# More all-ones filler products ahead of the prefix sums and ahead of tile 0's gather in an expert-routing kernel

## Chip, cores and metric

The kernel runs on one core of a Trainium2 chip. The metric is the device time of one execution in microseconds (us); lower is better. The engines that matter here are PE (TensorE, the matrix engine; PEld is its weight load), DVE (VectorE), ACT (ScalarE), POOL (GpSimd, which also issues the indirect transfers) and SP (which issues the plain ones).

## What is computed

A graph network of three levels on 625 nodes with 256 features, and then a mixture of experts on its result:

```python
x = x + gnn(layernorm(x), edge_index, ...)          # three edge convolutions, 20000 edges
xn = layernorm(x)
gate_scores = xn @ Wg + bg                          # 625 x 8
_, idx = top_k(gate_scores, 2)
mask = one_hot(idx, 8).sum(axis=-2)
h = gelu(einsum('td,edh->teh', xn, W1) + b1)        # 8 experts, 256 -> 512
y = einsum('teh,ehd->ted', h, W2) + b2              # 512 -> 256
out = x + einsum('ted,te->td', y, mask)
```

The kernel doesn't compute all eight experts for every node. It computes only the two that a node picks: it sorts the picks by expert into tiles of 128 rows ("slots"), gathers the rows of each tile, runs the tile's expert on it, and adds the result to the output rows.

## The kernel before, in words

Nodes are held as 5 tiles of 128. The program is written out by hand for each engine. Each engine runs its own list in order, and semaphores (`wait_ge`, `then_inc`) tie the lists together. All that stands in a list behind a waiting instruction waits too.

The last level of the graph part ends with `g_product` (lines 1340 to 1342, dense products). After it the routing stretch begins, some 14 us of small steps in which PE, DVE and ACT take turns. PE's list there is, in order:

- transposes of `x1_sb` (L1578) and the gate products of 8 columns (L1585), with `keep_clock(WARM_GATE)`, 6 fillers, between them;
- `keep_clock(WARM_ROUTE)`, fillers, at line 1601;
- a wait for `both_ready`: DVE has found the two best experts of each node (`best`, `best_id`, `pick`, `both_bf`, L1213 to L1223);
- the prefix sums: ten bf16 products of 8 to 40 columns (L1604, L1608, L1611) that count how many nodes ahead of each picked the same expert;
- `keep_clock(WARM_GATHER)`, fillers, at line 1652;
- `gather(0)` (L1622): 20 float32 products of 128 columns, which collect the rows of slot tile 0 with one-hot matrices (`hot_slot`) that DVE makes from the prefix sums (L1231 to L1240). It waits for `x2_f_done` (ACT has normalised the rows) and `hot_ready`;
- a wait for `experts_ready`, then a load of two expert numbers into PE's registers (L407), and `up(0, 0)` (L1629), the first expert product, which waits for `xt_ready`: ACT has copied the gathered tile from PSUM (L874);
- `gather(1)`, the same 20 products for slot tile 1, and a second load of expert numbers;
- `transpose_h(0)` (L1642), and ten products (L1665) that turn the slots into row numbers for the indirect transfers;
- the expert loop: per tile `transpose_h` (L1642), `up` (L1629), `transpose_x` (L1636), `down` (L1648), with each tile's rows fetched by an indirect transfer of POOL (L634) and its results added to the output by another (L640). Ten tiles are written out, the rest come from a loop with a run-time count.

The fillers are products whose result nobody reads. They go to `bank[3]`, which nothing uses in this stretch:

```python
def keep_clock(n):
    for _ in range(n):
        pe.matmul(bank[3][:, 0:P], ones_bf[:], ones_bf[:], start=True, stop=True)
...
keep_clock(WARM_ROUTE)
pe.wait_ge(both_ready, 1)
...
keep_clock(WARM_GATHER)
pe.wait_ge(x2_f_done, NT)
gather(0)
```

They wait for no semaphore, so PE starts them as soon as what stands ahead of them has been issued; what stands behind them waits until they are through.

## Time and profile before

| | us |
|---|---|
| median of 3 timed runs | 176.64 |
| the three runs | 175.98, 176.64, 177.07 |
| the profiled execution's own time | 177.76 |
| its span, first to last instruction | 175.9 |

The profile describes one execution. What lies around its span is 177.76 - 175.9 = 1.86 us. A duration from the trace is set against 177.76 us, not against the median. Rows give the start and length in us from the span's start, the engine, the source line, output and inputs, and the count of instructions. The granted clock (PEclk) is a share of full speed: 1.00 is 2.4 GHz and 0.50 is 1.2 GHz.

### The profile page before, as it was taken

How to read it: one execution, taken by the hardware profiler on the slowest of the kernel's cores; microseconds unless marked ns; L12 is line 12 of the kernel's file. 1: busy time of each engine (PE TensorE's matmuls, PEld its weight loads, DVE VectorE, ACT ScalarE, POOL GpSimd, SP SyncE). 2: the span in 40 equal slices, each digit the busy share in tenths (PEclk: the TensorE clock that was granted, in tenths of full speed). 3: DMA queues.
4: the chain of work that ended last, by engine and by line, in shares of the span. 5: the costliest groups of instructions: out<-in, count | busy, mean ns of one | idle time of the engine just before them, and what ended most of it. 6: DMA issues, size and time to landing. Idle time of an engine off the chain costs nothing.

```text
span 175.9 us, 3014 instructions
## 1 busy us (share of the span) xinstructions
PE 144.8 (82%) x958; PEld 121.4 (69%) x959; DVE 92.2 (52%) x245; ACT 63.9 (36%) x182; POOL 72.2 (41%) x95
## 2 busy tenths in 40 slices
PE   1443394999998899999999698989999999999710
PEld 1332273998798899999999686856666666766600
DVE  6699789768799891344139781622222222223100
ACT  8333975467212140312122640323433333343200
POOL 6605430000499049960001100075555666663661
PEclk9999997599999999999999958999999999999995
DMA  4679999996000699300000450024243333332332
GB/s 147 201 165 368 371 365 267 172 384 229 9 4 0 201 317 347 102 6 0 0 0 4 157 192 6 0 63 89 37 77 66 63 60 60 60 60 34 60 60 30
DMA packets 16983, 21.24 MB, mean 121 GB/s; under 512 B 1794, under 2 KB 13316, under 8 KB 16836
## 3 DMA queue, kind: packets, MB, share of 16 engines
q1 hardware_dynamic: 13764, 16.79, 29.4%
q0 software_dynamic: 3200, 4.20, 14.6%
q8 instruction: 12, 0.20, 0.4%
q14 instruction: 7, 0.06, 0.1%
HBM read 17.72 MB, written 3.26 MB: 119 GB/s over the span
## 4 chain that ended last, share of the span: by engine, by line
PE 58%; DVE 16%; DMA 11%; issue 5%; POOL 3%; ACT 2%; POOLq 1%; SPq 1%; ACTq 0%; DVEq 0%
PE cnt_ps L1648 9%; PE bank L1629 6%; DMA x_sb<-in_x 5%; PE bank L1505 4%; PE g_ps L1629 4%; PE cnt_ps L1642 3%; PE cnt_ps L1505 3%; PE bank L1622 3%; PE g_ps L1340 2%; PE g_ps L1341 2%; PE g_ps L1342 2%; DMA out_rows<-y_sb,row_of 2%; DVE a_hi L1038 2%; DMA out_rows<-y_sb,row_put 2%; DVE hot_lo L955 2%
## 5 line engine op out<-in xcount | busy, mean ns | idle before, releaser
L1648 PE MATMUL cnt_ps<-w_sb,h_t 128*128 x104 | 24.7, 380 | 1.2 <-ACT h_t L870 1.2
L1648 PEld LDWEIGHTS cnt_ps<-w_sb,h_t 128*128 128x128 f32 x104 | 18.8, 190 | 3.9 <-issue 1.9
L640 POOL DMA_INDIRECT out_rows<-y_sb,row_of x10 | 15.9, 1591 | 12.7 <-DMA out_rows<-y_sb,row_of 10.1
L634 POOL DMA_INDIRECT xg<-x_rows,row_of x12 | 12.0, 997 | 20.7 <-DVE row_of L1309 17.4
L1396 PE MATMUL bank<-hot_key,hot_lo 125*128 125x45 bf16 (+4 forms) x80 | 8.3, 244 | 11.2 <-DVE hot_key L958 7.2
L955 DVE TENSOR_TENSOR hot_lo<-iota_lo,edge_rel 125x1024 bf16<-125x1024 int16 x20 | 13.8, 690 | 3.0 <-PE g_ps L1396 2.9
L1396 PEld LDWEIGHTS bank<-hot_key,hot_lo 125*128 125x128 bf16 x80 | 5.2, 123 | 13.6 <-DVE hot_key L958 11.7
L1278 DVE TENSOR_TENSOR y_sb<-cnt_ps,b_bc 128x256 f32<-128x256 f32 x13 | 5.5, 425 | 17.3 <-PE cnt_ps L1648 17.3
L1629 PE MATMUL bank<-w_sb,xt 128*128 x28 | 13.4, 600 | 0.7 <-ACT xt L874 0.5
L1274 DVE TENSOR_TENSOR h_pre<-bank,b_bc 128x512 f32<-128x512 f32 x7 | 4.8, 692 | 16.0 <-PE bank L1629 16.0
L866 ACT ACTIVATE h_act<-h_pre 128x512 f32<-128x512 f32 x13 | 8.2, 629 | 9.7 <-DVE h_pre L1274 9.7
L1629 PE MATMUL g_ps<-w_sb,xt 128*128 x24 | 11.4, 596 | 0.0
L602 POOL IOTA key_tables<- 128x720 int16 x1 | 1.8, 1789 | 22.9 <-DVE a_hi L1038 22.9
L870 ACT COPY h_t<-cnt_ps 128x512 f32<-128x512 f32 x13 | 7.6, 585 | 9.7 <-PE cnt_ps L1642 9.6
L861 ACT COPY xt<-bank 128x256 f32<-128x256 f32 x12 | 4.5, 372 | 16.4 <-PE bank L1636 16.4
L1505 PE MATMUL bank<-a_hi,ys_hi 128*128 128x384 f32 x30 | 10.1, 338 | 0.0
L580 POOL TENSOR_TENSOR w_lo<-w_stage,w_hi 128x512 fp32r<-128x512 f32 x7 | 10.0, 1450 | 0.2
L1505 PE MATMUL bank<-a_hi,ys_lo 128*128 128x384 f32 x30 | 10.1, 336 | 0.0
L1396 PE MATMUL g_ps<-hot_key,hot_lo 125*128 125x45 bf16 (+4 forms) x80 | 8.5, 245 | 1.7 <-ACT a_hi L720 0.9
L1274 DVE TENSOR_TENSOR h_pre<-g_ps,b_bc 128x512 f32<-128x512 f32 x6 | 4.2, 692 | 10.5 <-PE g_ps L1629 10.5
L958 DVE TENSOR_TENSOR hot_key<-key_tables,edge_rel 125x360 bf16<-125x360 int16 (+4 forms) x20 | 8.9, 446 | 0.0
L1134 DVE SCALAR_TENSOR_TENSOR ut_lo<-bank,ut_hi 128x384 fp32r<-128x384 f32 x4 | 2.2, 558 | 12.5 <-ACT ut_hi L840 12.5
(289 smaller groups left out, 407.4 us busy)
## 6 DMA issues: line engine op xcount, KB each, us to landing
w_sb<-in_L_ffn_W SPq DMA_DIRECT2D x16, 512.0 KB, 9.6
b_bc<-in_L_ffn_b SPq DMA_DIRECT2D x8, 256.0 KB, 4.9
w_stage<-in_L_gnn_W SPq DMA_DIRECT2D x3, 512.0 KB, 5.7
w_stage<-in_L_gnn_Wf SPq DMA_DIRECT2D x4, 256.0 KB, 7.6
b_bc<-in_L_ffn_b SPq DMA_DIRECT2D x1, 1024.0 KB, 9.1
x_sb<-in_L_gnn_bf POOLq DMA_DIRECT2D x1, 640.0 KB, 14.3
x_rows<-x_f SPq DMA_DIRECT2D x1, 640.0 KB, 3.3
x_sb<-in_x SPq DMA_DIRECT2D x1, 512.0 KB
```

Of the source, the lines that this page charges most:

```text
L580: pool.tensor_tensor(w_lo[:, r, :, i * D:(i + 1) * D], part, w_hi[:, r, :, i * D:(i + 1) * D].bitcast(f32), ALU.subtract)\
L634: pool.indirect_dma_start(out=xg[:, b, :], out_offset=None, in_=x2_rows, in_offset=bass.IndirectOffsetOnAxis(ap=rows, axis=0)).then_inc(x_ ...
L640: pool.indirect_dma_start(out=out, out_offset=bass.IndirectOffsetOnAxis(ap=rows, axis=0), in_=y_sb[:, b, :], in_offset=None, compute_op=AL ...
L866: act.activation(h_act[:, h, :], h_pre[:, h, :], ACT.Gelu).then_inc(act_ready, 1)
L870: act.copy(h_t[:], bank[2].rearrange("p (k s) -> p k s", k=HC)).then_inc(h_t_ready, 1)
L955: dve.tensor_tensor(hot_lo[:, u % RING:u % RING + 2, :, :], iota_lo[0:EP].unsqueeze(1).broadcast_to((EP, 2, P, CT)), rel[:, 0].unsqueeze(2 ...
L958: dve.tensor_tensor(hot_keys(u, 2), turn_keys(u // UNROLL)[0:EP].rearrange("p n w i -> p (n w) i").unsqueeze(1) .broadcast_to((EP, 2, NT * ...
L1274: dve.tensor_tensor(h_pre[:, h, :], up_bank(h)[:, :], b1_bc[:, ds(e, 1), :], ALU.add).then_inc(pre_ready, 1)
L1396: last = pe.matmul(pane(k), hot_lo[:, u % RING, :, i], hot_keys(u)[:, 0, :, i], start=i == i0, stop=i == i0 + n_i - 1, skip_group_check=True)
L1505: step = pe.matmul(z_bank(i), y[:, u, m], a_t[:, u, cols], start=first and u == 0 and y is y_parts[0], stop=u == NT - 1 and y is y_parts[- ...
L1629: last = pe.matmul(up_bank(h)[:, :], xt[:, k, h * P:(h + 1) * P], w1_sb[:, ds(e, 1), k, :], start=k == 0, stop=k == KC - 1)
L1648: last = pe.matmul(bank[3][:, 0:D], h_t[:, k, :], w2_sb[:, ds(e, 1), k, :], start=k == 0, stop=k == HC - 1)
```

## The change

Two of the three counts of fillers grow: 40 in place of 22 ahead of the prefix sums, and 28 in place of 14 ahead of tile 0's gather. The six between the gate products stay. Nothing else differs.

```diff
-WARM_GATE, WARM_ROUTE, WARM_GATHER = 6, 22, 14
+WARM_GATE, WARM_ROUTE, WARM_GATHER = 6, 40, 28
```

## Rows read from the trace of the kernel before

**Rows 1.** The page: span, PE's busy tenths and the granted clock in 40 slices

```profile
span 175.9 us, 3014 instructions
PE   1443394999998899999999698989999999999710
PEclk9999997599999999999999958999999999999995
```

**Rows 2.** Chain that ended last, 100.5 to 108.2 us: start, length, what

```profile
100.54 0.21 DVE both_bf L1223
100.75 0.05 issue
100.80 0.21 PE bank L1604
101.01 0.09 PE bank L1608 x4
101.10 0.15 PE bank L1611 x5
...
102.33 0.57 DVE hot_slot L1240
102.90 0.14 issue
103.03 4.51 PE bank L1622 x20
...
107.56 0.38 ACT xt L874
107.94 0.13 issue
```

**Rows 3.** Chain that ended last, 108 to 113 us

```profile
108.07 1.98 PE bank L1629 x4
110.05 2.23 PE g_ps L1622 x20
```

**Rows 4.** Windows: stretch, length, busy of each engine, granted clock, DMA share, GB/s

```profile
99.40:100.40 1.00, 0.03 (x1) 0.00 (x0) 0.93 (x12) 1.00 (x4) 0.00 (x0) 1.00 0.18 52
100.40:100.50 0.10, 0.00 (x0) 0.00 (x0) 0.10 (x1) 0.10 (x2) 0.00 (x0) 0.74 0.15 51
103.00:107.20 4.20, 4.17 (x19) 4.20 (x20) 3.15 (x19) 0.00 (x0) 0.00 (x0) 0.50 0.42 146
107.30:107.60 0.30, 0.23 (x2) 0.03 (x1) 0.00 (x0) 0.04 (x1) 0.00 (x0) 1.00 0.00 0
```

**Rows 5.** PE's timeline around both runs of fillers

```profile
98.04 1.39 PE L1347 MATMUL cnt_ps<-ones_bf 128*128 128x128 bf16 x22
100.80 0.21 PE L1604 MATMUL bank<-both_bf,tri_bf 128*128 128x40 bf16 x1 [1.37 <-DVE both_bf L1223]
101.09 1.65 PE L1347 MATMUL cnt_ps<-ones_bf 128*128 128x128 bf16 x14
```

**Rows 6.** Windows in earlier stretches with gaps on PE, columns as in rows 4

```profile
29.00:32.00 3.00, 1.88 (x14) 1.88 (x14) 3.00 (x7) 0.78 (x4) 0.00 (x0) 0.50 1.14 215
56.00:60.00 4.00, 2.82 (x18) 2.62 (x17) 3.78 (x12) 0.81 (x2) 1.25 (x1) 1.00 0.26 78
```

**Rows 7.** PE's timeline at the gap of the second of them

```profile
57.81 0.45 PE L1340 MATMUL bank<-ut_hi,w_hi 128*128 128x384 f32 x1 [1.18 <-DVE ut_lo L1134]
```

**Rows 8.** DVE's timeline after the first one-hot matrices

```profile
104.85 0.13 DVE L1265 TENSOR_SCALAR pairs_i<-owner_i 1x1 int32<-1x1 int32 x1
105.17 0.82 DVE L1240 TENSOR_TENSOR hot_slot<-iota_p,place 128x640 f32<-128x640 f32 x1
106.17 0.18 DVE L1286 CAST tile_pos<-tile_pos_i 128x20 bf16<-128x20 int32 x1
```

**Rows 9.** Register loads and POOL's wait: duration ns min/median/max, first and last start

```profile
L407 PEldq TENSOR_LOAD <-owner_i x2: 553/1368/2183, 105.0 to 110.1; - x2
L630 POOLq EVENT_SEMAPHORE  x1: 17/17/17, 107.0 to 107.0; - x1
```

**Rows 10.** Chain that ended last, 105 to 176 us

```profile
114.65 2.85 DMA xg<-x_rows,row_of
...
155.75 0.44 DVE y_sb L1278
...
156.97 3.82 DMA out_rows<-y_sb,row_of
```

## The prediction

> **What bounds the kernel now.** I read the page first. Its clock line is 9 nearly everywhere and drops at two places, slices 7 and 8 and slices 24 and 25 [rows 1]. The second drop is where the change sits, because a slice is 4.4 us and the routing stretch lies at 94 to 108 us. Then I read the chain that ended last, since only time on it is worth anything. In the routing stretch it runs DVE (`both_bf`), the prefix sums on PE, DVE again (`hot_slot`), then 4.51 us of PE for `gather(0)`, then the copy of the tile on ACT [rows 2]. The fillers aren't on it at all. The same 20 products appear once more as `gather(1)`, and there the chain gives them 2.23 us [rows 3]. The windows say why: the clock is 1.00 until 100.4, falls to 0.50 there after a stretch in which PE was busy for 0.03 of 1.00 us, stays at 0.50 while the gather keeps PE full (4.17 of 4.20 us), and is back at 1.00 from 107.3 [rows 4]. So `gather(0)` runs whole at 1.2 GHz and `gather(1)` at 2.4 GHz. PE's own timeline shows the hole ahead of the fall: the 22 fillers start at 98.04 and are through at 99.43, and PE then idles 1.37 us for `both_bf` [rows 5].
>
> **Part 1, 18 more fillers ahead of the prefix sums.** 22 took 1.39 us at full clock [rows 5]. A single one overlaps its neighbours, so I take some 0.22 us for the last one's own length and (1.39 - 0.22) / 21 = 0.056 us for each step. 18 more are 1.00 us: the last ends at 100.43 and not at 99.43. The prefix sums can't start before `both_bf`, ready at 100.75 and used at 100.80 [rows 2]. That leaves 0.37 us of slack, so the direct cost is 0. The hole shrinks from 1.37 to 0.37 us. If the cover were gone (each of the 40 at the pace of half clock, where 14 took 1.65 us, so (1.65 - 0.22) / 13 = 0.11 us), they would end at 98.04 + 39 x 0.11 + 0.22 = 102.55 and hold the prefix sums up by 1.7 us. The bounds of this part are 0 and +1.7, and I take 0, by the row of the same fillers in the same place.
>
> A rule of the Trainium skill speaks against this: "TensorE: Matmul & The Clock Gate", section "Back-to-back issue gap", says that a sustained stream of weight loads and 128-column products keeps about 81 ns per product. By that, 40 would take about 3.3 us, end at 101.4 and delay the prefix sums by 0.6 us, and the second run would add 0.3 us. The 22 in place took 1.39 us with their weight loads, which is 63 ns each even with the tail counted, so the trace disagrees, and I go by the trace.
>
> **Part 2, the clock through the prefix sums and the gather.** If PE no longer stands empty for over a microsecond ahead of 100.4, the clock should stay up. No trace shows this stretch with 40, so I bound it. The clock stayed at 1.00 across 56 to 60 us, where PE was busy 2.82 of 4.00 us and had one gap of 1.18 us between dense products of 256 and 384 columns [rows 6, 7]. It was at 0.50 across 29 to 32 us, with 1.88 of 3.00 us busy [rows 6]. The new stretch has no gap longer than 0.4 us between 98 and 103, which lies well on the side of the stretch that held. What it's worth: `gather(0)` goes from 4.51 us to between 2.23 and 2.39 us (the second is the length on PE's timeline with the last product's tail). I take a gain of 2.2. The ten prefix products take 0.45 us of the chain at half clock [rows 2]. Their gain lies between 0 and half of it, 0.22 us. They are mostly fixed length (0.21 us for the first one), so I take 0.05.
>
> **Part 3, 14 more fillers ahead of the gather.** At full clock 28 take 27 x 0.056 + 0.22 = 1.73 us. They start at about 101.05 and end at 102.8. The gather waits for `hot_slot` until 102.90 and starts at 103.03 [rows 2], so there are 0.1 to 0.25 us of slack and the cost is 0. At half clock they would take 27 x 0.11 + 0.22 = 3.2 us, end at 104.3 and delay the gather by 1.25 us. The bounds are 0 and +1.25; I take 0, because it goes with part 2.
>
> **What is late next.** The gather would end at about 105.25 and the copy of the tile on ACT at 105.65. `up(0, 0)` needs two register values that PE can load only after `experts_ready`, that is after 104.98, and the load took 0.55 us [rows 8, 9]: ready at 105.6, so it is hidden by less than 0.1 us. The gain behind that point can't become larger than about 2.3 us without this load, or the second `hot_slot` (ready at 105.99, needed by `gather(1)` at about 107.8) [rows 8], being late. DVE is free at 106.35 for a product that now ends at about 107.9 [rows 8]. POOL's first indirect gather, now at 114.65 and then at about 112.4, has its stored rows at 107.0 [rows 9, 10]. From 114.65 on the chain is the transfers, PE's expert loop and the last scatters behind the last `y_sb` [rows 10], each started by the one before, so all of it moves up by the same amount.
>
> **The sum.** -2.2 - 0.05 + 0 + 0 = -2.25 us: 177.76 - 2.25 = 175.5 us, with a span of 173.65.
>
> **How that stands to the median.** The profiled execution is 1.12 us above the median and 0.69 us above the slowest timed run, and the three timed runs spread over 1.09 us. That is the size of part of what the clock costs here. I read it so that the clock's fall at this place differs in time and depth between executions: the profiled one paid for all of it, and the fastest timed one (175.98) for little. Then the changed kernel should come near or a little below the fastest run of before, and 175.5 agrees with that.
>
> **Rivals.**
> 1. *Every run of before paid the full price, and the profiled one is longer for another reason.* For it: one profile can't tell what the timed runs did. Against it: their spread. Then the gain comes off the median: 176.64 - 2.25 = 174.4 us. Chance 0.17.
> 2. *The clock mostly held already in the timed runs*, and their spread has another source, such as the earlier drop in slices 7 and 8 [rows 1], which the change doesn't touch. Then the time stays at 176.3 to 176.6. Chance 0.14.
> 3. *The fall comes earlier, ahead of or inside the route fillers.* The place is the gate stretch, 96 to 98 us, in which PE has only transposes and products of 8 columns, and which the change leaves as it is. For it: nothing makes this stretch denser. Against it: the clock was 1.00 up to 100.4 in the profile. Its price: a filler at half clock takes 0.11 and not 0.056 us, so from the seventh such filler on (0.37 / 0.054) the prefix sums are late, and with all 40 by 1.7 us. If the clock is back before the gather, the gather starts at 104.75 and takes 2.23 us, which is 0.6 us sooner than in the profile: 177.2. If the 28 run at half clock too, they end at 102.55 + 0.45 + 3.2 = 106.2, and a gather at full clock then ends at 108.4, 0.9 us later than the 107.54 of before: 178.7 us, slower than before. Between them 177.9. Chance 0.10, for all cases in which the clock falls in spite of the fillers.
> 4. *The fillers' own pace is slower than 0.056 us in a longer run.* At 81 ns the two parts would give 0.6 + 0.3 us back: 176.4 us. Against it stands the row of the 22. Chance 0.02.
>
> **How the numbers follow.** The forecast, 175.5 us, has 0.57; the rivals have 0.17, 0.14, 0.10 and 0.02. Its own range is 175.0 to 176.1. For 8 in 10 the range takes in rivals 1, 2 and 4 and the mildest of rival 3: 174.4 to 176.9. One per cent, 1.77 us, is about what a measurement of this kernel can tell from no change; the bounds are 174.9 and 178.4. Faster than that: most of rival 1 and a tenth of the forecast, 0.21. Slower: under half of rival 3, 0.04. The rest, 0.75, lies within.
>
> **What would show it.** The clock at 1.00 from 98 to 108 us; 40 fillers in about 2.4 us, ending before 100.5; the prefix sums still at 100.8; 28 fillers ending before 102.9; `gather(0)` in 2.2 to 2.4 us from about 103.0; `up(0, 0)` at about 105.8; the expert loop some 2.2 us earlier; a span near 173.7. I would be wrong if PEclk showed 0.50 anywhere from 97 to 107, if the wait of L1604 named no DVE step (the fillers are then late), or if `up(0, 0)` waited for the register load.

## The result and the profile after

The changed kernel takes 175.99 us in the median of 20 runs (175.29 to 177.46). The kernel before, in 20 runs beside it, takes 177.38 us (175.98 to 183.95). The ratio is 0.9925, with a 95% interval of 0.9903 to 0.9946: 0.75% faster, a gain clear of noise, and less than one per cent. Ratios here leave out executions over 1.5% above the fastest of their kernel (none of the changed kernel, four of the twelve of e3), so that a ratio can differ from the quotient of the medians. The profiled execution takes 176.38 us with a span of 174.6, where that of before took 177.76 with 175.9.

The page of the kernel after, to be laid beside [rows 1]: the second drop of the clock, in slices 24 and 25, has gone from the line, the first, in slices 7 and 8, has stayed, and PE is at 9 in slice 23, where it was at 6.

```profile
span 174.6 us, 3078 instructions
...
PE   1453394999699999999999988989999999999700
...
PEclk9999998599999999999999999999999999999985
```

PE's timeline of the kernel after, beside [rows 5]:

```profile
98.17 2.39 PE L1347 MATMUL cnt_ps<-ones_bf 128*128 128x128 bf16 x40
100.93 0.19 PE L1604 MATMUL bank<-both_bf,tri_bf 128*128 128x40 bf16 x1 [0.37 <-DVE both_bf L1223]
...
101.20 1.72 PE L1347 MATMUL cnt_ps<-ones_bf 128*128 128x128 bf16 x28
103.14 2.47 PE L1622 MATMUL bank<-hot_slot,x_f 128*128 128x128 f32 x20 [0.21 <-DVE hot_slot L1240]
106.15 1.98 PE L1629 MATMUL bank<-w_sb,xt 128*128 x4 [0.55 <-ACT xt L874]
```

The hole ahead of the prefix sums is 0.37 us where it was 1.37, both waits still name DVE (the fillers are never late), and `up(0, 0)` waits for ACT, not for its register load. The windows of the kernel after, beside [rows 4], show the clock at 1.00 through all of it:

```profile
97.00:98.00 1.00, 1.00 (x12) 1.00 (x10) 0.56 (x4) 0.48 (x2) 0.44 (x5) 1.00 1.01 341
98.00:103.00 5.00, 4.55 (x81) 4.21 (x80) 4.17 (x33) 3.97 (x7) 0.00 (x0) 1.00 0.34 107
103.00:107.30 4.30, 3.62 (x23) 2.98 (x24) 3.26 (x19) 0.46 (x2) 0.00 (x0) 1.00 0.45 158
```

The chain that ended last, in the kernel after, beside [rows 2], [rows 3] and [rows 10]:

```profile
100.93 0.19 PE bank L1604
101.13 0.09 PE bank L1608 x4
101.21 0.14 PE bank L1611 x5
...
103.14 2.48 PE bank L1622 x20
105.62 0.02 issue
105.64 0.38 ACT xt L874
...
106.15 1.98 PE bank L1629 x4
108.13 2.23 PE g_ps L1622 x20
...
153.82 0.44 DVE y_sb L1278
...
154.30 0.72 issue
155.03 0.24 POOLq L400
155.26 3.76 DMA out_rows<-y_sb,row_of
```

From profile to profile the account is: everything ahead of the fillers 0.13 us later (98.17 against 98.04), which is what is left of larger differences that come and go (a product that the kernel after starts at 51.59 us started 1.30 us sooner before, and one at 57.77 us 0.04 us later); the prefix sums 0.42 against 0.45 us; `gather(0)` 2.48 against 4.51 us; so `up(0, 0)` 1.92 us earlier (106.15 against 108.07); the last tile's `y_sb` 1.93 us earlier (153.82 against 155.75). Behind it 0.2 us are given back before the scatter starts (1.44 against 1.22 us from `y_sb` to the transfer) and another 0.2 in the last scatters, and the whole execution is 1.38 us shorter.

### The profile page after: what moved, and what is told of

Its sections match the earlier page's. It is cut to its first block, busy times and chain, and to the rows that moved or that the text cites. A ratio compares the mean times of both kernels' runs of the same rounds, so it can differ in the third digit from the quotient of the medians.

```text
span 174.6 us, 3078 instructions
## 1 busy us (share of the span) xinstructions
PE 144.1 (83%) x990; PEld 120.8 (69%) x991; DVE 91.6 (52%) x245; ACT 63.8 (37%) x182; POOL 72.1 (41%) x95
## 4 chain that ended last, share of the span: by engine, by line
PE 63%; DVE 14%; DMA 8%; issue 5%; ACT 4%; POOL 2%; POOLq 1%; ACTq 0%; DVEq 0%
PE cnt_ps L1648 9%; PE bank L1629 6%; PE bank L1505 6%; DMA out_rows<-y_sb,row_put 4%; PE g_ps L1629 4%; PE cnt_ps L1505 4%; DVE hot_lo L955 3%; PE g_ps L1340 3%; PE g_ps L1341 3%; PE g_ps L1342 3%; PE cnt_ps L1642 3%; DVE a_hi L1038 2%; DMA out_rows<-y_sb,row_of 2%; DVE hot_key L958 2%; PE cnt_ps L1340 2%
```

## The experiments

There are twelve experiments. e1 is the changed kernel itself, and the others differ from it in the counts of fillers, their shape, or one added run of fillers; e9 is the kernel of e3 once more. The kernel before ran beside each group on the same chip, since its median moves from chip to chip: 177.06 us beside e1 to e4, 177.24 beside e5 to e8 and 177.94 beside e9 to e12. The medians in the table are of all executions. For orientation (e9 is a single execution):

| | fillers | median us | ratio to before, 95% interval |
|---|---|---|---|
| e1 | 40, 28 | 176.03 | 0.9940 (0.9914 to 0.9967) |
| e2 | 40, 14 | 175.84 | 0.9931 (0.9905 to 0.9958) |
| e3 | 22, 28 | 176.86 | 0.9955 (0.9916 to 0.9993) |
| e4 | 0, 0 | 177.43 | 1.0031 (0.9999 to 1.0062) |
| e5 | 60, 28 | 176.52 | 0.9962 (0.9938 to 0.9987) |
| e6 | 80, 56, of 8 columns | 177.70 | 1.0029 (1.0000 to 1.0058) |
| e7 | 40, 28, early 18 | 174.32 | 0.9836 (0.9800 to 0.9871) |
| e8 | 40, 28, early 32 | 177.20 | 0.9966 (0.9930 to 1.0002) |
| e10 | 22, 14, early 18 | 175.01 | 0.9837 (0.9783 to 0.9892) |
| e11 | 40, 14, early 18 | 175.07 | 0.9834 (0.9786 to 0.9881) |
| e12 | 40, 28, early 10 | 176.86 | 0.9926 (0.9887 to 0.9964) |

**e1: the changed kernel again, beside its parts.** No edit.

> The changed kernel once more, beside its parts on one chip. Theory (the clock holds through prefix sums and the gather, and nothing else counts): clock 1.00 from 97 to 107 us, gather(0) 2.2 to 2.5 us on the chain, 1.0 to 1.6 us below the kernel before. Rival (the gain is a shift of chance in other stretches): the gain changes by over half, or gather(0) stays at 4.5 us in some executions.

Its profile has the clock at 1.00 through the stretch and 2.48 us for `gather(0)`, as the kernel after had; the gain here is 1.03 us in the median. The expectation is met, at its lower end.

**e2: only the 18 more ahead of the prefix sums.**

```diff
-WARM_GATE, WARM_ROUTE, WARM_GATHER = 6, 40, 28
+WARM_GATE, WARM_ROUTE, WARM_GATHER = 6, 40, 14
```

> 18 more fillers ahead of the prefix sums, the 14 ahead of the gather left. Theory A (the long hole ahead of the prefix sums was what brought the clock down): the whole gain, 1.0 to 1.6 us, gather(0) at 2.3 to 2.5 us. Theory B (the hole of 0.8 us between the end of the 14 and the gather, which opens once they run at full clock, brings it down a little later): half of the gain or less, and the clock falls between 102 and 104 us.

175.84 us, 1.22 below the kernel before: the whole gain. The profile has 2.48 us for the gather. Theory A holds: the first count does the work. The second added nothing that can be measured, although with 14 PE stands empty for 0.99 us ahead of the gather. The clock stayed at 1.00 across that hole here, and across the same one of 1.00 us in e11. PE's timeline of e2:

```profile
101.43 0.94 PE L1347 MATMUL cnt_ps<-ones_bf 128*128 128x128 bf16 x14
103.36 2.47 PE L1622 MATMUL bank<-hot_slot,x_f 128*128 128x128 f32 x20 [0.99 <-DVE hot_slot L1240]
```

**e3 and e9: only the 14 more ahead of the gather.**

```diff
-WARM_GATE, WARM_ROUTE, WARM_GATHER = 6, 40, 28
+WARM_GATE, WARM_ROUTE, WARM_GATHER = 6, 22, 28
```

> 14 more fillers ahead of the gather, the 22 ahead of the prefix sums left. Theory A: where the clock falls at 100.4 us the 28 run at half clock in 3.2 us, end near 104.3, and start the gather 1.2 us late; little gain, -0.5 to +0.3 us, or a loss in such executions. Theory B: a gain of 0.5 to 1.0 us, since the clock then falls less often and comes back sooner.

The twelve times go from 175.03 to 178.24 us, a spread of 3.2 us where the twelve of e1 have 1.8. Six are at 175.03 to 176.59 and six at 177.14 to 178.24; the upper six have mean granted clocks of 0.950 to 0.954, and five of the lower six have 0.971 to 0.982. The median of the twelve, 176.86, is 0.2 us below the kernel before, as Theory A has it; the ratio in the table stands on the eight shorter ones and flatters this kernel. The profiled execution took 175.24 us and had kept its clock, with the same 1.37 us hole that the kernel before has. Its PE timeline and a window over the hole:

```profile
97.20 1.39 PE L1347 MATMUL cnt_ps<-ones_bf 128*128 128x128 bf16 x22
99.95 0.19 PE L1604 MATMUL bank<-both_bf,tri_bf 128*128 128x40 bf16 x1 [1.37 <-DVE both_bf L1223]
...
102.16 2.47 PE L1622 MATMUL bank<-hot_slot,x_f 128*128 128x128 f32 x20 [0.22 <-DVE hot_slot L1240]
```

```profile
99.00:100.00 1.00, 0.05 (x2) 0.05 (x3) 0.90 (x8) 1.00 (x3) 0.00 (x0) 1.00 0.18 57
```

So with the same hole as in the kernel before the clock can be kept. That this kernel also loses it in other executions is what the spread of its times and their mean clocks suggest; a second profile was taken to catch that case.

> 22 and 28 fillers again, for one more profile: its twelve executions before spread from 175.0 to 178.2 us at mean clocks of 0.95 to 0.98, and the one with a profile had kept its clock. If the clock falls ahead of the prefix sums here, the 28 should take 3.0 to 3.2 us at half clock, end 1.2 us after hot_slot is ready, and the time be 177 to 178.3 us. If it doesn't, 28 take 1.7 us and the time is 175.0 to 176.4 us.

It was the kept case again: 175.99 us, 28 fillers in 1.72 us, gather in 2.47. The other case, in which the 28 should run at half clock and be late, has only the spread of times and the mean clocks behind it; no profile shows it.

**e4: no fillers at either place.**

```diff
-WARM_GATE, WARM_ROUTE, WARM_GATHER = 6, 40, 28
+WARM_GATE, WARM_ROUTE, WARM_GATHER = 6, 0, 0
```

> No fillers ahead of the prefix sums and of the gather; the six between the gate products stay. Theory: the clock falls in every execution ahead of or in the prefix sums, gather(0) takes 4 to 4.5 us, and the time is 0.5 to 1.5 us above the kernel before. Rival (fillers are of no use, the clock goes by the work itself): the same time as before, within 0.3 us.

177.43 us, 0.37 above the kernel before, just under the lower end of the theory's range (0.5) and just over the rival's bound (0.3), with an interval of the ratio that touches 1 (0.9999 to 1.0062). The profile shows the mechanism as the theory has it: a hole of 2.62 us, the clock falls inside it, and the gather takes 4.07 us.

```profile
100.32 0.21 PE L1604 MATMUL bank<-both_bf,tri_bf 128*128 128x40 bf16 x1 [2.62 <-DVE both_bf L1223]
...
102.55 4.05 PE L1622 MATMUL bank<-hot_slot,x_f 128*128 128x128 f32 x20 [1.80 <-DVE hot_slot L1240]
```

```profile
98.00:99.00 1.00, 0.00 (x0) 0.00 (x0) 0.92 (x10) 0.61 (x2) 0.00 (x0) 1.00 0.38 90
99.00:100.00 1.00, 0.00 (x0) 0.00 (x0) 0.96 (x11) 1.00 (x3) 0.00 (x0) 0.52 0.19 53
```

By the medians the 22 and 14 of before were thus worth some 0.4 us in all, which isn't clear of noise, and the change another 1.0 to 1.4, which is.

**e5: fillers that outlast the wait.**

```diff
-WARM_GATE, WARM_ROUTE, WARM_GATHER = 6, 40, 28
+WARM_GATE, WARM_ROUTE, WARM_GATHER = 6, 60, 28
```

> 60 fillers ahead of the prefix sums and 28 ahead of the gather. They should end at 98.0 + 59 x 0.056 + 0.22, that is 101.6, which is 0.7 us after DVE has both_bf. Theory (the 40 cost nothing because they end 0.37 us before that; filler time beyond it is paid in full): prefix sums 0.5 to 0.8 us later than with 40, time 0.5 to 0.8 us above the changed kernel, still 0.3 to 0.8 us below the kernel before. Rival (the sequencer hides them, or the longer run changes the clock): same time as the changed kernel.

176.52 us, 0.72 below the kernel before beside it, where e1 was 1.03 below: some 0.3 us of the gain is gone by the medians, with intervals that overlap. That is less than the 0.5 to 0.8 expected for the time, and only the profile tells the theory from its rival. The fillers have come onto the chain:

```profile
98.47 3.37 PE cnt_ps L1347 x60
101.83 0.02 PE bank L1604
101.85 0.09 PE bank L1608 x4
```

and the prefix sums start 3.35 us after the first filler (98.32 to 101.67) where they started 2.76 us after it with 40 (98.17 to 100.93): 0.59 us later, against 0.5 to 0.8 expected. 60 fillers took 3.51 us, 0.056 us for each step, so the pace holds in a longer run too.

**e6: as many microseconds of fillers, but of 8 columns.**

```diff
-WARM_GATE, WARM_ROUTE, WARM_GATHER = 6, 40, 28
+WARM_GATE, WARM_ROUTE, WARM_GATHER = 6, 80, 56
...
+                c = 8 if n > WARM_GATE else P
                 for _ in range(n):
-                    pe.matmul(bank[3][:, 0:P], ones_bf[:], ones_bf[:], start=True, stop=True)
+                    pe.matmul(bank[3][:, 0:c], ones_bf[:], ones_bf[:, 0:c], start=True, stop=True)
```

> 80 and 56 fillers of 8 columns in place of 40 and 28 of 128 columns: at about 30 ns each they keep PE's records busy as long (2.4 and 1.7 us), but stream a sixteenth of the columns per product. Theory A (what the products stream keeps the clock): the clock falls as without fillers, gather(0) 4 to 4.5 us, time 0.3 to 1 us above the kernel before. Theory B (that PE is issued something is enough): as the changed kernel, 1.0 us or more below the kernel before.

177.70 us, 0.46 above the kernel before, as with no fillers. PE's records are full (2.20 of 2.20 us in the first window), and yet the clock falls and the gather takes 4.09 us. It falls at 98.9 us, while the thin fillers run and 0.6 us before the hole opens at 99.50, so the hole, which is only 0.59 us, isn't what brought it down. PE's timeline and the windows of e6:

```profile
97.33 2.17 PE L1348 MATMUL cnt_ps<-ones_bf 128*128 128x8 bf16 x80
100.09 0.22 PE L1605 MATMUL bank<-both_bf,tri_bf 128*128 128x40 bf16 x1 [0.59 <-DVE both_bf L1223]
...
102.33 4.09 PE L1623 MATMUL bank<-hot_slot,x_f 128*128 128x128 f32 x20 [0.31 <-DVE hot_slot L1240]
```

```profile
97.30:99.50 2.20, 2.20 (x82) 2.12 (x81) 1.99 (x22) 1.34 (x3) 0.00 (x0) 0.87 0.39 110
98.80:98.90 0.10, 0.10 (x10) 0.10 (x8) 0.10 (x3) 0.10 (x1) 0.00 (x0) 1.00 0.05 10
98.90:99.00 0.10, 0.10 (x10) 0.10 (x8) 0.10 (x3) 0.10 (x1) 0.00 (x0) 0.57 0.15 31
99.50:105.70 6.20, 5.30 (x83) 5.24 (x83) 5.33 (x29) 2.72 (x5) 0.00 (x0) 0.50 0.43 148
```

So it isn't enough that PE has something to do; fillers of 128 columns held the clock here and fillers of 8 columns didn't. The gate stretch ahead of them, whose products have 8 columns too, kept its clock at 1.00 in every profile.

**e7, e8, e12: fillers at the first drop of the clock.** The other drop, slices 7 and 8, has PE on the chain too: in the kernel before, from 30 to 36 us, PE is busy for 5.88 of 6.00 us at a mean clock of 0.53, after 2 us of waiting for DVE's `hot_key`. These kernels put fillers into that wait, into the bank whose next content starts afresh anyway.

```diff
+WARM_EARLY = 18
...
             for u in range(20, 28, 2):
+                if u == 26:
+                    pe.wait_ge(consts, 6)
+                    pe.wait_ge(a_written, chunks_before(u) - PANES + 1)
+                    for _ in range(WARM_EARLY):
+                        pe.matmul(bank[0][:, 0:P], ones_bf[:], ones_bf[:], start=True, stop=True)
                 sum_pair(u)
```

> The changed kernel with 18 more fillers at about 28 us, ahead of unit 26 of the edge counts, where PE waits 2.0 us for DVE's hot_key and the clock is at half from about 29 to 34 or 36 us. At half clock 18 take 1.95 us and just fill the gap. Theory (PE is on the chain at half clock from 30 to 35 us): the clock is back up to 3 us sooner in a part of the executions, time 0.2 to 0.8 us below the changed kernel. Rival (DVE bounds the stretch): no change within 0.2 us.

174.32 us, 2.92 below the kernel before: 0.9836, the best of the study. Each against the kernel before beside it, that is 1.9 us better than the changed kernel in e1, and I had expected 0.2 to 0.8. The windows of e7: the clock comes back at 32.2 us, not at 35.6 to 35.7 as in the profiles before and after. That moment moves by itself: in the ten profiles with no early fillers or with ten of them it lies between 33.4 (e3) and 36.2 us (e12), but in the four with 18 or 32 it is never later than 32.2. In e8, e10 and e11 the products of 256 columns behind the fillers, from 31.4 to 32.0 us on, already take 0.28 us each, the length at full clock.

```profile
29.00:32.00 3.00, 3.00 (x26) 2.94 (x24) 3.00 (x6) 0.78 (x4) 0.00 (x0) 0.50 1.26 203
32.00:36.00 4.00, 4.00 (x37) 3.72 (x36) 2.50 (x6) 2.71 (x11) 0.00 (x0) 0.97 0.97 175
```

> The same with 32: 1.8 us at full clock, 3.4 us at half. Theory: where the clock is up at 28 us it stays up and some 2 us of the stretch are saved; where it is down the fillers delay the edge counts by 1.4 us and bring the clock up sooner, so that the two nearly cancel. Between 1.0 us below and 0.3 us above the changed kernel. Rival (DVE bounds the stretch): 0 to 1.4 us above it.

177.20 us, level with the kernel before beside it and so 1.0 us worse than the changed kernel in e1, outside the theory's upper end of 0.3 and inside the rival's 0 to 1.4. The fillers do end late, and the edge counts start at 31.22, not 30.03 as with 18. But that isn't what this profile lost, since the clock is back sooner: the product that the kernel after starts at 35.58 us starts here at 34.91. The first line below is of the kernel after, the others of e8:

```profile
35.58 0.38 PE L1342 MATMUL g_ps<-ht_hi,w_lo 128*128 128x384 f32 x1
...
28.39 2.99 PE L1434 MATMUL bank<-ones_bf 128*128 128x128 bf16 x32 [0.40 <-ACT a_hi L721]
31.22 0.49 PE L1397 MATMUL bank<-hot_key,hot_lo 125*128 125x85 bf16 x4
...
34.91 0.34 PE L1343 MATMUL g_ps<-ht_hi,w_lo 128*128 128x384 f32 x1
...
75.53 0.44 PE L1341 MATMUL bank<-ut_hi,w_hi 128*128 128x384 f32 x1 [2.22 <-issue]
```

The loss is the last line. At 71.7 us of the kernel after e8 is still 1.19 us ahead of it, and at this product it is 1.19 us behind: far from any filler PE stands idle for 2.22 us, and for the last 1.36 of them the chain names nothing that it waits for. One profile can't say whether such a gap or the late fillers make e8's median, so why 32 gave less than 18 stays open. Other profiles have such gaps too: the kernel after 1.44 us on PE ahead of a product at 47.65 us, and the chains of the kernel before, of e2, e5 and e9 a gap of 1.07 to 1.10 us, marked "issue" as well, at 49.1 to 49.4 us, this one between two steps of DVE. What causes them isn't settled.

> The changed kernel with 10 early fillers in place of 18 or 32: 1.1 us at half clock, so they leave about 0.5 us of the gap empty and can't delay the edge counts. Theory (it is the filled gap that brings the clock up sooner): between the changed kernel (176.0) and the one with 18 (174.3), near 175. Rival (18 is better only because less code shift happened to suit it): equal to 18 or to none.

176.86 us, 1.08 below the kernel before beside it, ratio 0.9926: no better than the change alone, where the theory had about 175. In the profile 0.60 us of the wait stays empty and the clock stays at half until 36.2 us. Ten did nothing that can be measured, 18 did. The times alone don't exclude the rival "only the code's place counts", but the clock in the traces speaks for the filled gap.

**e10 and e11: 18 early fillers with the counts of before, and with 40 and 14.** The early run itself is that of e7. Of e10 against the kernel before, and of e11 against the changed kernel:

```diff
 WARM_GATE, WARM_ROUTE, WARM_GATHER = 6, 22, 14
+WARM_EARLY = 18
```

```diff
-WARM_GATE, WARM_ROUTE, WARM_GATHER = 6, 40, 28
+WARM_GATE, WARM_ROUTE, WARM_GATHER = 6, 40, 14
+WARM_EARLY = 18
```

> The 18 early fillers alone, on the kernel before (22 and 14). Theory (the two clock stretches are independent): 1.0 to 1.9 us below the kernel before, as the early ones gave beside the change. Rival (they helped only together): under 0.5 us.

> The 18 early fillers with 40 and 14. The second half of the change gave nothing on its own beside the first, so this should equal the version with 28: 173.7 to 174.6 us. Were the 28 what makes sure of the gather's clock, the time would spread by 1 to 2 us more.

175.01 and 175.07 us, 2.93 and 2.87 below the kernel before on the same chip. Both expectations fail in part. e10 gave more than the 1.0 to 1.9 expected, and e11, with the first half of the change in it, gave no more than e10. By sums, 0.9925 for the change and 0.9837 for e10 should have made some 0.976, and no version got there; the intervals are half a per cent wide on either side, so what the change is still worth beside the early fillers is between nothing and most of its own gain. That is open.

The profile of e10 holds the most useful view of the late stretch: a short fall. The hole is 1.37 us as ever, the clock goes down at 99.3 and is back at 102.7, in the middle of the gather, which takes 3.16 us. PE's timeline and windows:

```profile
99.05 0.19 PE L1610 MATMUL bank<-both_bf,tri_bf 128*128 128x40 bf16 x1 [1.37 <-DVE both_bf L1224]
...
101.26 3.16 PE L1628 MATMUL bank<-hot_slot,x_f 128*128 128x128 f32 x20 [0.29 <-DVE hot_slot L1241]
```

```profile
99.30:102.70 3.40, 3.11 (x28) 2.87 (x25) 2.93 (x15) 1.87 (x3) 0.00 (x0) 0.50 0.67 238
102.70:105.00 2.30, 1.75 (x16) 1.56 (x15) 1.74 (x10) 0.37 (x1) 0.00 (x0) 1.00 0.08 28
```

## Why the prediction was right, point by point

The forecast was 175.5 us in 174.4 to 176.9; the median is 175.99, and the gain lies within 1%, as the likeliest class had it.

- *Where the time was.* Right: the clock over `gather(0)`. It is the one term of the chain that moved, 4.51 to 2.48 us.
- *Part 1, the fillers' price.* Right: 40 took 2.39 us (2.4 forecast), the hole shrank to 0.37 us (0.37), the cost was 0. e5 shows the bound on its other side: beyond the slack each filler is paid for.
- *The 81 ns of the Trainium skill* ("TensorE: Matmul & The Clock Gate", "Back-to-back issue gap"). The trace doesn't agree: the 40 took 60 ns each with the tail and the 60 took 59. Rival 4 falls.
- *Part 2, the clock.* Right in the direction. The size of the gather's term was too large: 2.03 us in place of 2.2, as `gather(0)` needs 2.48 us at full clock where `gather(1)` needs 2.23. Most of the difference is that the 2.23 leaves out what `gather(1)` does while the chain still counts `up(0, 0)`; on PE's timeline it takes 2.39, the nearer bound. The rest is the start: the first product of `gather(0)`, behind an empty PE, takes 0.35 us and the others 0.27. The reason that I gave, the length of the hole, was at most half of it: e3 and e9 have the same 1.37 us hole and keep the clock, e10 has it and loses the clock briefly, and in e6 the clock falls before its hole opens.
- *Part 3.* Right in cost: 28 took 1.72 us (1.73) and ended before `hot_slot`. In worth it was nothing that can be measured beside part 1 (e2). Alone it gave 0.2 us in the median of all twelve, with a wide spread (e3).
- *What is late next.* Nothing was, as said. `up(0, 0)` waited for ACT.
- *"All of it moves up by the same amount."* This step failed, by 0.4 us: `y_sb` of the last tile moved by 1.93 us and the end by 1.52.
- *How the profile stands to the median.* Here the forecast could have been far off, and the reading held, though not by the sign that it rested on. The profiled execution was slower than all three timed runs, 1.12 us above their median, but that was chance: it is 0.38 us above the median of 20, and seven of the 20 are slower than it. What bears the reading out is this: the profiled execution of before had paid the full price (4.51 us), while with the same 1.37 us hole others pay in part (3.16 us in e10) or not at all (e3, e9). The mean granted clocks say it too: a profile with both drops on record reads 0.950, those with one on record 0.964 to 0.979. Of the 75 executions of the kernel before beside the experiments 22 are under 0.96, of the 50 of the changed kernel, e2 and e5 none. The 22 are a lower bound, since e4 and e6, which lost the clock for the whole gather, read 0.967 and 0.965. The gain of the median is 1.39 us, the gain from profile to profile 1.38, both short of the 2.25 predicted for an execution with the full fall. For the median that is what a price that isn't always paid would give. For the profiles it is the terms above: -2.03 - 0.03 + 0.13 + 0.41 makes -1.52 for the chain's end, and from there to the end of the execution 5.57 us pass where 5.43 had, which leaves -1.38. Rival 1, a gain of the full 2.25 us off the median, falls; rival 2, that nothing was to be had, falls too; rival 3 was not seen in any profile with 40 fillers.
- *The sizes.* For the profiled execution 175.5 us was forecast and 176.38 measured. The 0.88 us are 0.19 of the gather and the prefix sums, 0.13 of a later start of the whole stretch, 0.41 of the tail and 0.14 behind the chain's end. Only the first of them belongs to the change and its stretch; the second arose ahead of the first added filler.

## What to carry to other kernels

Where dense PE work follows a stretch of small steps, compare a product's pace there with the same product's pace elsewhere, and look at the granted clock of that window before touching the work itself. Fillers were free here as long as they ended before the wait that follows them was over, and 60 of them, which didn't, held the prefix sums up by 0.59 us (e5); count the slack at full clock (0.056 us for 128 columns here) and check what a filler at half clock (0.11 us) would do. They were of use at 128 columns and of none at 8, too few did little (10 at 28 us), and one profile of such a kernel shows one draw of the clock, so its price is judged from many timed runs.

## What the runs showed of the hardware that I had not expected

- The same instructions with the same 1.37 us hole kept the clock at 1.00 in two profiles of one kernel, and with 22 and 14 fillers it was lost for 3.4 us in one profile (e10) and for 6.8 us in another (the kernel before). The fall comes and goes between executions.
- 80 products of 8 columns in 2.17 us, with PE's records full, didn't hold the clock (e6), which fell at 98.9 us in the midst of them; 40 of 128 columns in 2.39 us did, in every profile with them.
- The clock line and the windows, and with them the mean clock, count the stretch ahead of the first record of the clock as full. In e9 the windows give 1.00 from 29 to 32 us, while the products of 256 columns there take 0.41 us each, as they do at 0.50 elsewhere, and 0.28 at full clock. Early in a trace the products' own length is the safer witness.
- Gaps with no wait that the profile shows, 1.1 us on DVE at the same place in four profiles and 1.4 and 2.2 us on PE in one profile each, lie beside the clock as a candidate for the run-to-run spread. Their cause stays open.
